# Causal masks on TensorE: eight 64 by 64 tiles per four banks in place of sixteen 32 by 32 tiles

## The chip, the cores and the metric

One core of a Trainium2 chip runs the whole program. The metric is the device time of one execution in microseconds. Three executions of the kernel before took 2279.23, 2272.83 and 2267.55 us; the median is 2272.83 us.

## What is computed

The input is x with 32 batches of 128 tokens by 512 values, and a context of the same shape. Per batch, four residual stages follow each other:

```python
x = x + wkv(w, u, layernorm(x), ctx)              # decayed running sums over the tokens
x = x + attention(layernorm(x))                   # 16 heads of 32, causal: s <= t only
x = x + mlstm(layernorm(x), ctx, ctx)             # 16 heads, causal matrix exp(log_D)
x = x + experts(layernorm(x))                     # top 8 of 32 experts
# attention: scores = where(causal, q k^T * scale, lowest); softmax over s
# mlstm:     log_D  = where(lower triangle, F_t - F_s + i_s, -inf)
```

The two `where` lines are what the change is about. A large negative number is put in PSUM at every place outside the triangle, and the scores are then added onto it.

## The kernel before, in words

**Two phases.** The first (about the first 1130 us) is a software pipeline over the batches: in step j, batch j is in stage 0, batch j-1 in stage 1, and so on up to stage 5. Steps 0 to 5 and 32 to 36 are written out, and steps 6 to 31 (26 of them) are one loop. The second phase runs the experts and has no masks.

**Order by hand.** The instructions of each engine within a step stand in an order fixed by hand (`step` of each engine), and the engines meet through semaphores. Every engine works strictly down its own list.

**Masks.** `masks(bank, mask)` (L1188 to L1194) fills four PSUM banks of 128 partitions by 512 values with the causal mask. It multiplies pieces of the identity with pieces of a mask table (bfloat16). Each matmul streams 512 columns: 128 columns of the table, repeated for four heads. A matmul that reads SBUF partitions of row group i and writes PSUM partitions of column group q uses only the corner (i, q) of the TensorE array. Before, there are four row groups and four column groups of 32, so the sixteen matmuls of one call use sixteen different corners. Bank r of column group q takes row group (q + r) mod 4, and the tables are turned by as much.

**Its three callers in a step**, in PE's order:
1. `scores` (L1247, stage 1): masks in banks 0 to 3, then 16 products of q and k (L1251). PE waits for `head_norm_ready` ahead of it (L1415, L1416). DVE's `row_max` (L1696) waits for its end, and PE goes on to `gates` (L1258) and `centre` (L1264).
2. `scores_turned` (L1279, stage 1): masks in banks 0 to 3, then L1283. `minus_max` (L1290), `v` (L1296 to L1298), `y_turn`, `row_sums` (L1306) and `weighted_v` (L1314) come after it on PE. ACT's four exponentials wait for `minus_max`.
3. `log_d` (L1317, stage 2): masks in banks 4 to 7, then four products (L1321). PE waits ahead of it for ACT's `lt_part`, for POOL's `spread_sums` (L618) and for ACT's `log_row_sums` (L1484, L1485). ACT's `exp_log_d3` (L939) waits for its end at L1129 (L1130 takes the semaphore down). `qk` (L1329) is PE's last work of the step.

**After that**, in the next step, PE waits for `exp_log_d3` (L1341, L1342), then does `z_turn` (L1164), `project` (L1201 to L1204) and the rest. POOL issues eight indirect DMAs (`store_pair`, L557) per step from step 5 on; the last three follow `spread_sums` directly.

Of the kernel before, what the change touches and what calls it, by code (L numbers as in the profile page):

```python
# [21 lines left out]
def build(nc, x, ctx_in, small, eye, fixed, fixed_half, gate_rows, Wa, Wp, ln_scale, gate_w, w_gate, w_up, w_down, out,  # L22
          NB=None, NE=None):
    B, T, D = x.shape
# [25 lines left out]
    with ExitStack() as whole:  # L50
# [6 lines left out]
        ps = whole.enter_context(nc.psum_tensor("ps", [P, 8, 512], F32))  # L57
# [29 lines left out]
        with ExitStack() as ctx:  # L87
# [21 lines left out]
            identb, ustrict = half_t[:, 0:P], half_t[:, P:2 * P]  # L109
# [1046 lines left out]
            def _(pe):  # L1156
# [29 lines left out]
                                  start=True, stop=True)  # L1186

                def masks(bank, mask):  # L1188
                    for q_ in range(4):
                        for r in range(4):  # L1190
                            i = slice(32 * ((q_ + r) % 4), 32 * ((q_ + r) % 4) + 32)
                            pe.matmul(ps[32 * q_:32 * q_ + 32, bank + r, :], identb[i, i],
                                      mask[i, r, :].unsqueeze(1).to_broadcast([32, 4, T]),
                                      start=True, stop=False, skip_group_check=True)  # L1194

                def z_turn():
# [50 lines left out]
                def scores():  # L1247
                    masks(S_BANK, mask_ts)
                    for c in range(4):
                        for r in range(4):  # L1250
                            m = pe.matmul(ps[:, S_BANK + r, c * T:(c + 1) * T], qs[32 * r:32 * r + 32, c, :],  # L1251
                                          ks[32 * r:32 * r + 32, c, :], start=False, stop=True, skip_group_check=True)
                    return m
# [25 lines left out]
                def scores_turned():  # L1279
                    masks(S_BANK, mask_st)  # L1280
                    for c in range(4):
                        for r in range(4):
                            m = pe.matmul(ps[:, S_BANK + r, c * T:(c + 1) * T], ks[32 * r:32 * r + 32, c, :],  # L1283
                                          qs[32 * r:32 * r + 32, c, :], start=False, stop=False, skip_group_check=True)
                    return m
# [32 lines left out]
                def log_d():  # L1318
                    masks(LD_BANK, mask_st)
                    for r in range(4):  # L1320
                        m = pe.matmul(ps[:, LD_BANK + r, :], Lt[32 * r:32 * r + 32, :],  # L1321
                                      Rt[32 * r:32 * r + 32, :, :].rearrange("p c t -> p (c t)"),
                                      start=False, stop=True, skip_group_check=True)
                    return m
# [1294 lines left out]
def fixed_tables(np, bi, bf):  # L2619
    h, dh = bi.shape[0], 32  # L2620
    rows = np.arange(P)
    q, n = rows // 32, rows % 32
    cols = np.arange(P)
    pick = np.zeros((P, 4, P), np.float32)
    gsel = np.zeros((P, 2, P), np.float32)
    cmat = np.zeros((P, P), np.float32)
    bmat = np.zeros((P, 4, dh + 1), np.float32)
    side = np.zeros((P, 9), np.float32)
    for p in range(P):
        if n[p] < 4:  # L2630
            pick[p, n[p], :] = 1.0
        for r in range(4):
            for j in range(8):
                for m in range(2):
                    if n[p] == h * m + r + 4 * (j % 4):
                        gsel[p, m, 32 * r + j] = 1.0
        cmat[p, 32 * q[p]:32 * q[p] + dh - 1] = -1.0 / dh
        if n[p] < dh - 1:
            cmat[p, p] = 1.0 - 1.0 / dh
            bmat[p, q[p], n[p]] = 1.0  # L2640
            bmat[p, q[p], dh - 1] = -1.0
        else:
            bmat[p, q[p], dh] = 1.0
        if n[p] < 4:
            side[p, 0], side[p, 3] = 1.0, 1.0
        elif n[p] < 8:
            side[p, 1], side[p, 2] = 1.0, -1.0
        if n[p] < 8:
            side[p, 5 + n[p] % 4] = 1.0
    side[0:h, 4:5] = bi.reshape(h, 1)  # L2650
    side[h:2 * h, 4:5] = bf.reshape(h, 1)
    table = np.concatenate([pick.reshape(P, 4 * P), gsel.reshape(P, 2 * P), cmat, bmat.reshape(P, 4 * (dh + 1)), side], axis=1)
    one, low = 0x3F80, 0xF14A
    half = np.zeros((P, 10, P), np.uint16)
    half[rows, 0, rows] = one
    half[:, 1, :][cols[None, :] > rows[:, None]] = one
    for i in range(4):
        for r in range(4):
            for p in range(32):
                t = 32 * ((i - r) % 4) + p  # L2660
                half[32 * i + p, 2 + r, :][cols > t] = low
                half[32 * i + p, 6 + r, :][cols < t] = low
    return table, half.reshape(P, 10 * P)


# [34 lines left out]
```

How the kernel before makes its waits and increments, by code:

```python
            def scale_rows(eng, k, part, step):  # L433
                part_of = [[wdst[:, (part + j) // 2, ((part + j) % 2 * 2 + n) * P:((part + j) % 2 * 2 + n + 1) * P]
                            .rearrange("p (h d) -> p h d", h=H) for n in range(2)] for j in range(2)]
                for j in range(2):
                    eng.tensor_tensor(scaled_heads(k, j)[:, :, 0:DS], main_columns(k, j), scale(j, 0, DS), ALU.mult)
                    eng.tensor_tensor(part_of[j][0], low_columns(k, 1 - j), scale(j, 1, R), ALU.mult)
                    a = eng.tensor_tensor(part_of[j][1], low_columns(k, j), scale(j, 2, R), ALU.mult)
                a.then_inc(step, 1)
                eng.wait_ge(step, 1)
                eng.sem_inc(step, -1)
                for j in range(2):
                    a = eng.tensor_tensor(scaled_heads(k, j)[:, :, DS:DH], part_of[j][0], part_of[j][1], ALU.add)
                return a
# [23 lines left out]
                def load_x(i):  # L470
                    sp.wait_ge(first_residual_ready_for_sp, 1)
                    sp.sem_inc(first_residual_ready_for_sp, -1)
                    sp.dma_start(xt[:, :], x[bass.ds(i, 1)].rearrange("a p d -> p (a d)")).then_inc(x_loaded, 16)
# [1 line left out]
                def load_ctx(i):  # L475
                    sp.wait_ge(ctx_turn_ps, 1)
                    sp.sem_inc(ctx_turn_ps, -1)
                    sp.dma_start(ct[:, :], ctx_in[bass.ds(i, 1)].rearrange("a p d -> p (a d)")).then_inc(ctx_loaded, 16)
```

## Time and profile before

| what | value |
|---|---|
| median of three executions | 2272.83 us |
| the profiled execution | 2280.1 us |
| its span, first to last instruction | 2278.3 us |
| PE busy | 2008.4 us (88%) |
| DVE, ACT, POOL busy | 1581.6, 1203.3, 1534.6 us |
| mean granted TensorE clock | 0.964 |

The profiled execution is 7.3 us above the median of the three; 1.8 us of it lie outside the span. A line of the trace names the engine, the line of the kernel, the operation and the tiles. A number in square brackets behind it is the time the engine sat idle just before, with what ended it: `PEq L1416` is PE's own instruction queue, which was waiting at line 1416. The granted clock is 1.00 at 2.4 GHz and 0.50 at 1.2 GHz.

### The profile page before, as it was taken

What the parts mean: (1) busy time and instruction counts of PE and PEld (TensorE: products, weight loads), DVE (VectorE), ACT (ScalarE), POOL (GpSimd) and SP (SyncE); (2) the same over time, 40 slices, a digit from 0 to 9 for tenths busy, and PEclk for the clock granted to TensorE, in tenths of its full rate; (3) what the DMA queues carried; (4) which work ended last, traced back from release to release, by engine and by line L of the source; (5) the groups of instructions that cost most, each with busy time, mean ns of one, the idle gap of its engine ahead of it and who ended that gap; (6) DMA issues with size and microseconds to landing.
All of it is one profiled execution on the core that took longest, in us unless ns stands there. A gap on an engine that the chain in (4) does not pass through costs nothing. (4 is left out here: it accounts for less than half of the span.)

```text
span 2278.3 us, 66587 instructions
## 1 busy us (share of the span) xinstructions
PE 2008.4 (88%) x22279; PEld 1459.6 (64%) x22280; DVE 1581.6 (69%) x3262; ACT 1203.3 (53%) x3018; POOL 1534.6 (67%) x1622
## 2 busy tenths in 40 slices
PE   2899999999899899998748999999999999999986
PEld 2676666666666666666426776676776777767664
DVE  6688877877777777876445775777666667666663
ACT  3576556566656655665424554555454445554542
POOL 4247766766766776776667777777776777776764
PEclk9999999999999999999869999999999999999998
DMA  3111001001101000001028787777887878786874
GB/s 118 44 39 39 28 28 37 28 28 37 30 25 37 31 29 33 33 28 40 20 59 175 165 183 157 166 166 155 177 170 165 165 166 179 166 169 134 180 143 79
DMA packets 136030, 219.47 MB, mean 96 GB/s; under 512 B 28032, under 2 KB 61184, under 8 KB 135936
## 3 DMA queue, kind: packets, MB, share of 16 engines
q0 software_dynamic: 73472, 139.82, 32.0%
q1 hardware_dynamic: 57856, 70.17, 9.8%
q10 hardware_dynamic: 4608, 8.39, 1.0%
q8 instruction: 39, 0.64, 0.1%
q14 instruction: 55, 0.45, 0.1%
HBM read 133.07 MB, written 96.73 MB: 101 GB/s over the span
## 5 line engine op out<-in xcount | busy, mean ns | idle before, releaser
L2268 POOL DMA_INDIRECT out_dram<-y,m_add x300 | 498.4, 1661 | 218.1 <-POOLq L2276 156.4
L2418 PE MATMUL ps<-xh,wh 128*128 128x256 f16 (+1 forms) x1752 | 381.4, 267 | 6.4 <-PEq L2430 4.7
L2419 PE MATMUL ps<-xh,wl 128*128 128x256 f16 (+1 forms) x1752 | 381.4, 267 | 1.6 <-issue 1.6
L557 POOL DMA_INDIRECT slot_scratch<-pair,slots x248 | 295.0, 1190 | 79.2 <-issue 55.8
L2260 POOL DMA_INDIRECT xg<-z_scratch,slot_t x260 | 264.5, 1017 | 84.6 <-issue 75.6
L2499 ACT ACTIVATE y<-ps,wts_now 128x512 f32<-128x512 f32 x294 | 185.5, 682 | 148.0 <-ACTq L2498 123.5
L2423 PE MATMUL ps<-xl,wh 128*128 128x256 f16 (+1 forms) x1752 | 229.0, 267 | 2.5 <-PEq L2434 2.0
L2573 DVE SCALAR_TENSOR_TENSOR hx<-ps,s 64x256 f16<-64x256 f32 x146 | 62.2, 426 | 235.4 <-issue 131.1
L2418 PEld LDWEIGHTS ps<-xh,wh 128*128 128x128 f16 x1752 | 171.8, 98 | 52.8 <-issue 24.3
L2515 ACT ACTIVATE xh<-ps 128x512 f16<-128x512 f32 x146 | 87.2, 597 | 217.6 <-ACTq L2514 184.8
L2419 PEld LDWEIGHTS ps<-xh,wl 128*128 128x128 f16 x1752 | 171.8, 98 | 29.4 <-issue 0.8
L2423 PEld LDWEIGHTS ps<-xl,wh 128*128 128x128 f16 x1752 | 164.4, 98 | 24.4 <-issue 6.5
L2380 PE MATMUL ps<-ident,xg 128*128 128x128 f32 x1040 | 136.5, 275 | 31.0 <-DMA xg<-z_scratch,slot_t 27.3
L2398 PE MATMUL ps<-dh,hx 128*128 128x512 f16 x294 | 112.4, 382 | 41.5 <-PEq L2395 37.5
L2380 PEld LDWEIGHTS ps<-ident,xg 128*128 128x128 f32 x1040 | 116.9, 141 | 35.6 <-DMA xg<-z_scratch,slot_t 28.4
L2582 DVE CAST xh<-ps 128x512 f16<-128x512 f32 x146 | 100.0, 685 | 31.8 <-DVEq L2581 24.8
L2574 DVE SCALAR_TENSOR_TENSOR h<-ps,s 64x256 f32<-64x256 f32 (+1 forms) x292 | 121.5, 416 | 0.0
L2406 PE MATMUL ps<-dh,hh 128*128 128x512 f16 x294 | 113.7, 387 | 7.8 <-PEq L2403 3.4
L2590 DVE TENSOR_TENSOR xl<-ps,xh 128x512 f16<-128x512 f32 x146 | 100.9, 691 | 21.5
L2522 ACT ACTIVATE s<-ps 64x256 f32<-64x256 f32 x146 | 55.1, 378 | 113.0 <-ACTq L2521 102.0
L2407 PE MATMUL ps<-dl,hh 128*128 128x512 f16 x294 | 113.8, 387 | 0.0
L2401 PE MATMUL ps<-dl,hx 128*128 128x512 f16 x294 | 112.6, 383 | 0.0
(342 smaller groups left out, 5165.3 us busy)
## 6 DMA issues: line engine op xcount, KB each, us to landing
wst<-in_L_ffn_w_gate_dram SPq DMA_DIRECT2D x32, 384.0 KB
wst<-in_L_ffn_w_up_dram SPq DMA_DIRECT2D x32, 384.0 KB
xt<-in_x_dram SPq DMA_DIRECT2D x32, 256.0 KB
ct<-in_ctx_dram SPq DMA_DIRECT2D x32, 256.0 KB, 2.6
out_dram<-x SPq DMA_DIRECT2D x32, 256.0 KB
z_scratch<-zn ACTq DMA_DIRECT2D x32, 256.0 KB, 2.0
wdst<-in_L_ffn_w_down_dram SPq DMA_DIRECT2D x32, 256.0 KB
out_dram<-y,m_add POOLq DMA_INDIRECT x300
```

What stands on the lines that cost most here:

```text
L557: pool.indirect_dma_start(out=slot_d[:, :], out_offset=bass.IndirectOffsetOnAxis(ap=slots[:, k:k + 1], axis=0), in_=pair[:, k, :], in_offs ...
L2260: pool.indirect_dma_start(out=xg[b][:, h, :], out_offset=None, in_=z_d[:, :], in_offset=bass.IndirectOffsetOnAxis(ap=rows(h), axis=0)).the ...
L2268: pool.indirect_dma_start(out=acc_d[:, :], out_offset=bass.IndirectOffsetOnAxis(ap=m_add[:, k, h:h + 1], axis=0), in_=y[:, k, h, :], in_of ...
L2380: m = pe.transpose(ps[:, bank, c0:c0 + P], xg[b][:, h, k * P:(k + 1) * P], ident[:, :])
L2401: pe.matmul(o, hx2[:, t], dl[:, j, 1, :], start=False, stop=False)
L2406: pe.matmul(o, hh1[:, t], dh[:, j, 0, :], start=False, stop=False)
L2407: pe.matmul(o, hh1[:, t], dl[:, j, 0, :], start=False, stop=False)
L2418: pe.matmul(ps[:, dst, 0:cols], wh[:, j, k, c0:c0 + P], xh[:, k, 0:cols], start=(k == 0), stop=False)
L2419: pe.matmul(ps[:, dst, 0:cols], wl[:, j, k, c0:c0 + P], xh[:, k, 0:cols], start=False, stop=False)
L2423: m = pe.matmul(ps[:, dst, 0:cols], wh[:, j, k, c0:c0 + P], xl[:, k, 0:cols], start=False, stop=(k == KC - 1))
L2499: act.activation(y[:, k, h, :], ps[:, 5 + h, :], ACT.Copy, scale=wts_now[:, h:h + 1])\
L2574: dve.scalar_tensor_tensor(full, up, 1.0 / WSC, s, ALU.mult, ALU.mult).then_inc(dve_step, 1)
```

## The change

The loops run over two row groups and two column groups of 64 in place of four and four of 32. One call still fills four whole banks, with eight matmuls, each with 512 columns. The mask tables, built on the host, are turned to match; their size stays as it was. Nothing else differs.

```diff
                 def masks(bank, mask):
-                    for q_ in range(4):
+                    for q_ in range(2):
                         for r in range(4):
-                            i = slice(32 * ((q_ + r) % 4), 32 * ((q_ + r) % 4) + 32)
-                            pe.matmul(ps[32 * q_:32 * q_ + 32, bank + r, :], identb[i, i],
-                                      mask[i, r, :].unsqueeze(1).to_broadcast([32, 4, T]),
+                            i = slice(64 * ((q_ + r) % 2), 64 * ((q_ + r) % 2) + 64)
+                            pe.matmul(ps[64 * q_:64 * q_ + 64, bank + r, :], identb[i, i],
+                                      mask[i, r, :].unsqueeze(1).to_broadcast([64, 4, T]),
                                       start=True, stop=False, skip_group_check=True)
...
-    for i in range(4):
+    for i in range(2):
         for r in range(4):
-            for p in range(32):
-                t = 32 * ((i - r) % 4) + p
-                half[32 * i + p, 2 + r, :][cols > t] = low
-                half[32 * i + p, 6 + r, :][cols < t] = low
+            for p in range(64):
+                t = 64 * ((i - r) % 2) + p
+                half[64 * i + p, 2 + r, :][cols > t] = low
+                half[64 * i + p, 6 + r, :][cols < t] = low
```

## Rows read from the trace of the kernel before

**Rows 1.** The page, first part: busy time of each engine.

```profile
PE 2008.4 (88%) x22279; PEld 1459.6 (64%) x22280; DVE 1581.6 (69%) x3262; ACT 1203.3 (53%) x3018; POOL 1534.6 (67%) x1622
```

**Rows 2.** Windows: stretch, length, busy (count) by engine, PE clock, DMA share, GB/s.

```profile
240.00:1080.00 840.00, 764.47 (x11161) 543.69 (x11145) 639.99 (x1342) 500.11 (x1287) 578.53 (x795) 0.95 0.10 32
...
624.55:627.95 3.40, 3.40 (x11) 1.17 (x10) 2.92 (x7) 3.02 (x10) 1.13 (x3) 0.50 0.20 77
523.75:527.10 3.35, 3.35 (x19) 1.89 (x20) 3.00 (x7) 3.23 (x12) 1.22 (x2) 1.00 0.21 79
220.90:224.00 3.10, 3.10 (x19) 1.61 (x17) 3.10 (x8) 2.98 (x10) 0.96 (x3) 1.00 0.22 85
```

**Rows 3.** One line's instructions: row_max (L1696) in the loop of 26 steps.

```profile
L1696 DVE TENSOR_REDUCE nm<-ps x26: 2290/2292/2294, 204.2 to 1048.2; 128x16 f32<-128x2048 f32 x26
```

**Rows 4.** Timeline of DVE, row_max of six steps: start, length, idle before.

```profile
204.16 2.29 DVE L1696 TENSOR_REDUCE nm<-ps 128x16 f32<-128x2048 f32 x1 [1.04 <-DVEq L2024]
236.50 2.29 DVE L1696 TENSOR_REDUCE nm<-ps 128x16 f32<-128x2048 f32 x1 [1.03 <-DVEq L2024]
...
508.12 2.29 DVE L1696 TENSOR_REDUCE nm<-ps 128x16 f32<-128x2048 f32 x1 [1.04 <-DVEq L2024]
539.76 2.29 DVE L1696 TENSOR_REDUCE nm<-ps 128x16 f32<-128x2048 f32 x1 [1.05 <-DVEq L2024]
573.69 2.29 DVE L1696 TENSOR_REDUCE nm<-ps 128x16 f32<-128x2048 f32 x1 [1.04 <-DVEq L2024]
607.72 2.29 DVE L1696 TENSOR_REDUCE nm<-ps 128x16 f32<-128x2048 f32 x1 [1.05 <-DVEq L2024]
```

**Rows 5.** Timeline of PE in one step of the loop.

```profile
605.88 0.44 PE L1192 MATMUL ps<-half_t 32*32 32x512 bf16 x16 [0.76 <-PEq L1416]
606.25 1.17 PE L1251 MATMUL ps<-ks,qs 32*128 32x128 f32 x32
...
610.93 0.43 PE L1192 MATMUL ps<-half_t 32*32 32x512 bf16 x16
611.30 1.17 PE L1283 MATMUL ps<-qs,ks 32*128 32x128 f32 x32
...
613.39 0.38 PE L1296 MATMUL ps<-wvh,xnh 128*128 128x512 f16 x1
613.61 0.38 PE L1297 MATMUL ps<-wvl,xnh 128*128 128x512 f16 x1
...
618.92 0.44 PE L1192 MATMUL ps<-half_t 32*32 32x512 bf16 x16 [0.35 <-PEq L1485]
619.29 1.14 PE L1321 MATMUL ps<-Rt,Lt 32*128 32x512 f32 x8
620.50 1.59 PE L1329 MATMUL ps<-qT,kT 32*128 32x128 f32 x26
...
624.05 0.63 PE L1164 MATMUL ps<-ident,zn 128*128 128x128 f32 x4 [0.62 <-PEq L1342]
```

**Rows 6.** Timeline of ACT and POOL in the same step.

```profile
623.16 0.60 ACT L939 ACTIVATE dm<-ps 128x512 f32<-128x512 f32 x1 [2.09 <-ACTq L1130]
...
617.58 1.04 POOL L618 TENSOR_TENSOR Rt<-nx,fixed_t 128x512 f32<-128x512 f32 x1
...
620.16 0.96 POOL L557 DMA_INDIRECT slot_scratch<-pair,slots  x1 [0.30 <-issue]
621.43 0.96 POOL L557 DMA_INDIRECT slot_scratch<-pair,slots  x1 [0.30 <-issue]
```

**Rows 7.** Timeline of PE: start of qk and of z_turn in two other steps.

```profile
216.94 0.94 PE L1329 MATMUL ps<-qT,kT 32*128 32x128 f32 x21
...
220.52 0.63 PE L1164 MATMUL ps<-ident,zn 128*128 128x128 f32 x4 [0.52 <-PEq L1342]
...
520.91 1.57 PE L1329 MATMUL ps<-qT,kT 32*128 32x128 f32 x28
...
523.75 0.63 PE L1164 MATMUL ps<-ident,zn 128*128 128x128 f32 x4 [0.52 <-PEq L1342]
```

## The prediction, made before the changed kernel ran

> **What bounds the kernel now.** I read the page first: PE is busy 88% of the span [rows 1]. Masks are laid only in the first phase, so I cut out its loop of 26 steps. PE is busy 764 of 840 us there, and the granted clock averages 0.95, not 1.00 [rows 2]. The reader is to see two things: PE has little idle time to give, and its clock is not always full. Next come the step lengths, from one `row_max` to the next. 26 of them start between 204.2 and 1048.2 us [rows 3], so 25 intervals average 33.76 us. They are of three kinds [rows 4]: 34.03 us (573.69 to 607.72), 31.64 us (508.12 to 539.76) and 32.34 us (204.16 to 236.50). In the first kind the clock is 0.50 for 3.4 us at the start of `project`; in the other two it is 1.00 at that place [rows 2]. Going through the loop step by step I find two intervals of the short kind and one of the middle kind; from the mean of 33.76 the other 22 then average 34.0. With the last step that makes 23 low stretches, which agrees with the mean clock: 0.95 over 840 us, rounded, stands for 22 to 27 stretches of 3.4 us at 0.50 [rows 2].
>
> What sets the end of a step I take from the timelines [rows 5, 6]. PE waits 0.76 us before `scores`, 0.35 before `log_d` and 0.62 before `z_turn`. The striking one is ACT: the four products of `log_d` are streaming from 619.29, and `qk` follows at 620.50, yet ACT waits for the end of `log_d` until 623.16, after 2.09 us idle. POOL's last two indirect DMAs run from 620.16 to 622.39 in that time. Whatever holds the release back, it comes some 2 us after the arithmetic, and the next step (`z_turn` at 624.05) hangs on it.
>
> **The price of one call.** Sixteen matmuls start almost together: one lasts about 0.38 us and the group 0.44, so the last starts 0.06 after the first. The next group starts 0.37 after the first start, in all three calls [rows 5]. That is one round of 512 columns (0.215 us between 512-column matmuls, 613.39 to 613.61) plus about 0.1 us of changing over. In the changed code the corners of the array come in this order, as (row group, column group): (0,0) (1,0) (0,0) (1,0) (1,1) (0,1) (1,1) (0,1). If starts keep program order, the third has to wait for the first; the fifth and sixth go with the third and fourth; the seventh waits for the fifth. That makes three rounds in place of one: two more at 0.215, less 0.05 since fewer starts follow each other in the last round. I take +0.38 us per call. The bounds: one round, if nothing conflicts, -0.03; two rounds +0.17; all eight in a row +1.45 (seven more times 0.215, less 0.05).
>
> A rule that bears on this: the Trainium skill, "TensorEngine Tiling (Array Packing)", Tiling Modes, gives the array four independent tiles at 64 by 64. Eight matmuls would then be two rounds, +0.17 us per call. The Trainium skill, "TensorE: Matmul & The Clock Gate", Part 3, says that matmuls start in program order; by that it is three. The trace agrees with the latter only so far as no matmul in it starts ahead of an earlier one; no row has a call in which a corner is used twice.
>
> **Where the calls stand.** *First call (`scores`).* PE starts it when a wait ends, and DVE waits 1.05 us for its end [rows 4]. `gates` and everything DVE, ACT and POOL do for the gates come after it, down to POOL's `spread_sums` at 617.58 and the indirect DMAs behind it [rows 6]. So +0.38 passes to the whole step. The least is 0 (if `head_norm` came earlier, which nothing gives), the most 0.38.
>
> *Second call (`scores_turned`).* PE has no idle time around it, so `minus_max`, `v`, the exponentials, `row_sums` and with them ACT's logarithm, for which PE waits before `log_d`, are 0.38 later. *Third call (`log_d`).* Another 0.38. Both together put the products of `log_d` from 619.29 to 620.05 (counted without the first call), and their end to about 621.2. That is still ahead of 623.16, when ACT went on [rows 6]. `qk` moves from 620.50 to about 621.25; at its pace without gaps (L1251, 1.17 us for the same work) it would end at 622.4. The cover is the late release, nearly 2 us of it. POOL's DMAs do not wait for these two calls. I take 0 for both; if the cover is gone, 0.76 per step. Below nothing is open too: in the step at 508.12 `z_turn` came 2.84 us after `qk` started, against 3.55 in the common step [rows 5, 7], so a release 0.7 us earlier occurs.
>
> *Count.* 26 steps of the loop times 0.38 is 9.9 us. Outside it there are 96 - 78 = 18 calls. In steps 1 to 4 no indirect DMA runs, so nothing hides the 11 calls there. Of the 7 others I count 5 (the first of step 5, three of step 32, one of step 33). 16 times 0.38 is 6.1. Sum +16.0 us. The host's tables have the same size and cost nothing; 24 fewer matmuls per step shorten only PE's queue.
>
> **The clock.** A low stretch costs 34.0 - 32.34 = 1.65 us. Before it, PE is sparse: `qk` starts at 620.50, runs with gaps, and `z_turn` starts at 624.05. The second and third call push the dense work 0.75 us into that hole. The distance from `qk` to `z_turn` becomes about 2.8 us, as in the step at 508.12 that kept its clock (2.84). Against that, the step at 204.16 kept its clock with 3.58 [rows 7]. So the hole alone does not decide, and its place in time counts too. None of the 23 stretches or all of them may go: 0 to -38 us. I take 8, since neither end has more than a row or two for it: -13.2 us.
>
> **Sum.** +16.0 - 13.2 = +2.8 us, on 2280.1 us for the profiled execution. That one stands 7.3 us above the median; on 2272.83 it makes 2275.6 us.
>
> **Rivals.**
> - *Forecast, mixed clock.* Between 2 and 14 stretches go: +12.7 to -7.1, or 2266 to 2286 us. Chance 0.34.
> - *Slower: the clock falls as often as now.* Place: the hole before `z_turn`. Price: the full +16.0, 2288.8 us; and, if the cover of the second and third call is gone in the loop, 52 times 0.38 more (+19.8), 2308.6 us. It decides when fewer than 3 stretches go, or when 0.3 us of the two later calls passes to each step. For it: the hole begins later but ends at the same semaphore, and steps 0.38 us longer may fall on low stretches just as often. Against it: denser PE work where the clock is decided. Chance 0.34.
> - *Faster: the clock holds.* All 23 go: 16.0 - 38.0 = -22 us, 2250.9. If the release also comes 0.7 us earlier in each step, because `log_d` ends at a better moment between POOL's DMAs, 2232.7. For it: the 2.84 us above, in a step of 31.64. Against it: two short steps in 25 are little. Chance 0.22.
> - *The change does not do what it says.* With two rounds, each passing call costs 0.17: 42 calls, +7.1 us; with 8 stretches gone, -6.1, or 2266.7 us. Chance 0.08. All eight in a row: 42 times 1.45, +61 us, 2334 us. For it speaks no row, since matmuls in different corners overlap now. Chance 0.02.
>
> **How the numbers follow.** A measurement of this kernel can tell about 0.5%, 11.4 us, from no change. Faster takes the third case and a part of the two rounds (0.25); the same, the forecast and the rest (0.39); slower, the second and the last (0.36). For 8 in 10 I leave out all eight in a row, the earliest release in every step, and the full loss of cover: 2248 to 2304 us. The likeliest case's own range is 2266 to 2286. The predicted time is 2276 us.
>
> **What would show it.** Eight L1192 matmuls of 64 by 64 per call in starts of 2, 4 and 2, about 0.215 apart, and the next group 0.75 after the first start (0.54 for two rounds). `qk` 0.7 to 0.8 us later against `row_max`, with ACT's wait at L1130 shorter by about as much and its end unmoved. Steps with a full clock of 32.7 us, with a low one 34.4. The number of stretches at 0.50 in the loop, 23 now, decides the sign: 15 is the forecast, 20 or more is slower, under 10 faster. The forecast is wrong in its mechanism if `qk` ends later against `spread_sums` by more than 0.3 us and `z_turn` with it, or if the calls keep to 0.4 us.

## The result, and the profile after

The changed kernel takes 2217.36 us, the median of four executions (2215.52 to 2220.25); the kernel before took 2276.03 us on the same chip (four executions, 2267.55 to 2282.05). The ratio is 0.9746, with a 95% interval of 0.9722 to 0.9771: 59 us faster, outside the range of the prediction on its fast side. The profiled execution took 2215.52 us, its span 2213.6 us, with a mean granted clock of 0.983.

The first part of the page after, against [rows 1]:

```profile
PE 1966.0 (89%) x21511; PEld 1438.6 (65%) x21512; DVE 1581.0 (71%) x3262; ACT 1206.7 (55%) x3018; POOL 1534.8 (69%) x1622
```

768 matmuls are gone (96 calls, eight fewer in each), and PE is busy 42 us less. DVE, ACT and POOL do what they did. Two windows of the loop, against [rows 2] (the second lies at the start of `project`, where the common step had its clock at 0.50):

```profile
240.00:1080.00 840.00, 766.23 (x11037) 551.93 (x11035) 666.74 (x1427) 526.86 (x1348) 614.70 (x857) 0.99 0.11 34
313.00:316.40 3.40, 3.38 (x18) 1.83 (x19) 2.28 (x5) 2.83 (x11) 1.44 (x3) 1.00 0.08 30
```

Of the 23 low stretches of the loop one is left. DVE, ACT and POOL do 4 to 6% more in the same 840 us: the steps are shorter. DVE's timeline, `row_max` of two steps, against [rows 4]:

```profile
298.17 2.29 DVE L1696 TENSOR_REDUCE nm<-ps 128x16 f32<-128x2048 f32 x1 [1.08 <-DVEq L2024]
329.25 2.29 DVE L1696 TENSOR_REDUCE nm<-ps 128x16 f32<-128x2048 f32 x1 [1.08 <-DVEq L2024]
```

31.08 us, where the common step had 34.03. From the first `row_max` of the loop to the one after the loop it was 878.4 us (204.2 to 1082.6) and is 817.1 us (205.0 to 1022.1). These 61.3 us are nearly all of the 64.6 between the two profiled executions. PE's timeline of that step, against [rows 5]:

```profile
301.36 0.63 PE L1192 MATMUL ps<-half_t 64*64 64x512 bf16 x8
301.92 1.17 PE L1283 MATMUL ps<-qs,ks 32*128 32x128 f32 x32
...
309.33 0.63 PE L1192 MATMUL ps<-half_t 64*64 64x512 bf16 x8 [0.34 <-PEq L1485]
309.90 1.14 PE L1321 MATMUL ps<-Rt,Lt 32*128 32x512 f32 x8
310.91 1.59 PE L1329 MATMUL ps<-qT,kT 32*128 32x128 f32 x32
313.02 0.79 PE L1164 MATMUL ps<-ident,zn 128*128 128x128 f32 x4 [0.52 <-PEq L1342]
```

Two things are to be seen. A call hands over after 0.56 us, not 0.37: the price is +0.19 us. And `qk` is no longer strung out: it takes 1.59 us where it took up to 3, and `z_turn` starts 2.11 us after it, not 3.55. ACT's and POOL's timelines of the same step, against [rows 6]:

```profile
312.13 0.60 ACT L939 ACTIVATE dm<-ps 128x512 f32<-128x512 f32 x1 [0.65 <-ACTq L1130]
```

```profile
308.00 1.04 POOL L618 TENSOR_TENSOR Rt<-nx,fixed_t 128x512 f32<-128x512 f32 x1
309.19 1.08 POOL L557 DMA_INDIRECT slot_scratch<-pair,slots  x1 [0.16 <-issue]
310.58 0.96 POOL L557 DMA_INDIRECT slot_scratch<-pair,slots  x1 [0.30 <-issue]
```

ACT now goes on 4.13 us after `spread_sums` began; before it was 5.58 us (623.16 less 617.58). In both kernels three indirect DMAs follow `spread_sums`; the view above shows the first two, [rows 6] the last two. Measured from the end of `log_d`'s last product (the profile models the ends of matmuls), the release comes 0.95 us late (median of 26 steps) where it came 2.60 us late. ACT's waits at L1130 in the loop, first of the kernel before, then after (total us, times, longest):

```profile
ACT dm L939 <- ACTq L1130: 52.7, 26, 2.1
```

```profile
ACT dm L939 <- ACTq L1130: 20.3, 25, 2.0
```

So the late release, which the prediction used as cover, is what shrank.

### The profile page after: what moved, and what is told of

Read it like the earlier page. It is cut to its first block and busy times, and to the rows that moved or that the text cites. A ratio compares the mean times of both kernels' runs of the same rounds, so it can differ in the third digit from the quotient of the medians.

```text
span 2213.6 us, 65051 instructions
## 1 busy us (share of the span) xinstructions
PE 1966.0 (89%) x21511; PEld 1438.6 (65%) x21512; DVE 1581.0 (71%) x3262; ACT 1206.7 (55%) x3018; POOL 1534.8 (69%) x1622
```

## Experiments

The runs were made in five series, each with the kernel before beside it: 1 (e1, e3, e4, e7), 2 (e2, e5, e6, e8), 3 (c1 and the runs with f), 4 (with g), 5 (with h). The series fell on two conditions of the machine, and this matters for all that follows. In series 1 and 3 the kernel before took 2283.6 and 2281.6 us, as in the first measurement. In series 2, 4 and 5 it took 2130.6, 2130.1 and 2129.2 us. The first are called **slow-release** series, the others **prompt-release** series, after what their traces show. "Lag" is the time from the end of `log_d`'s last product to its semaphore; "qk" is the time from its first start to its last end; both are medians of the 26 loop steps. Low stretches are counted in the loop. Most expectations were written for a kernel before of 2280 us, and some name a kind of chip; chip 0 gave both series 3 (slow-release) and series 4 (prompt-release), so the number of the chip does not decide the condition. Where a run fell in a prompt-release series, what they say of releases and low stretches had no object, and only the price of the masks and of moved work could be read.

| run | ratio to before (95%) | step | lag | qk | low |
|---|---|---|---|---|---|
| *slow-release:* before, profiled | | 33.98 | 2.60 | 2.95 | 23 |
| changed, profiled | 0.9746 (0.9722 to 0.9771) | 31.08 | 0.95 | 1.56 | 1 |
| e1_split16 | 1.0001 (0.9970 to 1.0032) | 33.82 | 2.50 | 3.12 | 16 |
| e3_third64 | 0.9757 (0.9710 to 0.9803) | 31.17 | 1.01 | 1.62 | 1 |
| e4_moved | 0.9821 (0.9772 to 0.9869) | 31.65 | 0.04 | 1.17 | 1 |
| e7_shift | 1.0025 (1.0001 to 1.0050) | 34.06 | 2.39 | 3.04 | 20 |
| c1_changed | 0.9801 (0.9761 to 0.9841) | 31.64 | 1.73 | 2.32 | 0 |
| f5_firsttwo64 | 1.0069 (1.0032 to 1.0105) | 34.06 | 2.71 | 3.13 | 25 |
| f8_split16b | 1.0039 (0.9998 to 1.0080) | 34.07 | 2.48 | 3.12 | 18 |
| f2_whole4 | 0.9908 (0.9879 to 0.9936) | 32.33 | see there | 1.07 | 0 |
| *prompt-release:* g0_changed | 1.0011 (0.9997 to 1.0024) | 29.79 | 0.04 | 1.17 | 0 |
| e5_firsttwo64 | 1.0015 (1.0002 to 1.0028) | 29.72 | 0.04 | 1.17 | 0 |
| e8_split16b | 1.0017 (1.0003 to 1.0031) | 29.69 | 0.04 | 1.17 | 0 |
| e2_whole4 | 1.0143 (1.0120 to 1.0166) | 30.41 | 0.04 | 1.07 | 0 |
| g1_changed_moved | 1.0194 (1.0163 to 1.0225) | 31.27 | 0.04 | 1.17 | 0 |

### Is it the tiles or the number of matmuls?

The 64 by 64 tiles stay, but each matmul is cut into two of 256 columns, so that a call has sixteen again. In e1 both halves carry the start flag, and its masks do not stay whole under the scores. In e8 and f8 (one edit, two series; the diff) only the first half carries it, and the masks stay whole.

```diff
-                            pe.matmul(ps[64 * q_:64 * q_ + 64, bank + r, :], identb[i, i],
-                                      mask[i, r, :].unsqueeze(1).to_broadcast([64, 4, T]),
-                                      start=True, stop=False, skip_group_check=True)
+                            for h_ in range(2):
+                                pe.matmul(ps[64 * q_:64 * q_ + 64, bank + r, 256 * h_:256 * h_ + 256], identb[i, i],
+                                          mask[i, r, :].unsqueeze(1).to_broadcast([64, 2, T]),
+                                          start=(h_ == 0), stop=False, skip_group_check=True)
```

> The changed kernel with each 64 by 64 mask matmul cut in two of 256 columns: sixteen matmuls per call again, the same tiles and the same columns in all. Theory A (the number of TensorE instructions ahead of qk is what counts: qk and the release of log_d are held up by a supply or completion path that falls behind while POOL issues its indirect DMAs): the gaps in qk come back, qk takes 2.4 to 2.9 us from its first start to its last end instead of about 1.5, the release of log_d lags its arithmetic by over 2 us in most steps, loop steps are above 33 us and the kernel is within 0.7% of the kernel before. Theory B (tile shape and array work count: larger tiles keep the clock and shorten what follows): steps stay at 31.0 to 31.2 us and the kernel at 2215 to 2222 us.

> As e1_split16, but only the first of the two halves of a bank carries the start flag, so that the masks stay whole. Theory A: as there, the lag of the release about 2.5 us and qk about 3.1 us in most steps, 2265 to 2285 us. If the time of e1_split16 came from its second start flags and not from the count, this one is as fast as the changed kernel, 2215 to 2225 us.

> The kernel of e8_split16b again (64 by 64 tiles, each matmul cut in two of 256 columns, sixteen per call). On a chip of the first kind, theory A: lag about 2.5 us, qk about 3.1 us, within 0.7% of the kernel before; theory B: as fast as the changed kernel. On a chip of the second kind: 1.000 to 1.003.

PE's timeline of a step of e1, then DVE's `row_max` of two pairs of steps:

```profile
313.80 0.66 PE L1193 MATMUL ps<-half_t 64*64 64x256 bf16 x16 [0.27 <-PEq L1483]
314.38 1.14 PE L1322 MATMUL ps<-Rt,Lt 32*128 32x512 f32 x8
315.38 0.90 PE L1330 MATMUL ps<-qT,kT 32*128 32x128 f32 x18
316.48 0.47 PE L1330 MATMUL ps<-qT,kT 32*128 32x128 f32 x2 [0.20 <-issue]
317.20 0.51 PE L1330 MATMUL ps<-qT,kT 32*128 32x128 f32 x5 [0.26 <-issue]
317.96 0.52 PE L1330 MATMUL ps<-qT,kT 32*128 32x128 f32 x7 [0.25 <-issue]
```

```profile
237.84 2.29 DVE L1697 TENSOR_REDUCE nm<-ps 128x16 f32<-128x2048 f32 x1 [1.10 <-DVEq L2025]
270.25 2.29 DVE L1697 TENSOR_REDUCE nm<-ps 128x16 f32<-128x2048 f32 x1 [1.10 <-DVEq L2025]
...
469.36 2.29 DVE L1697 TENSOR_REDUCE nm<-ps 128x16 f32<-128x2048 f32 x1 [1.12 <-DVEq L2025]
503.43 2.29 DVE L1697 TENSOR_REDUCE nm<-ps 128x16 f32<-128x2048 f32 x1 [1.14 <-DVEq L2025]
```

The call takes 0.58 us, practically as in the changed kernel, on the same corners and with the same columns, and still the whole gain is gone, in e1 and in f8. Tiles and array time are not the cause; the number of matmuls (each with its weight load) is. The rows also show a second sign of it: `qk` runs 18 products without a gap and then comes in driblets, with idle time that no wait explains ("issue"). Counted from the first mask on, PE got 16 + 8 + 18 = 42 matmuls without a gap. In the changed kernel `qk` comes to its first such gap (over 0.18 us from one start to the next) after 26 to 31 products in most steps of the two slow-release traces, in the step shown after 29, which is 8 + 8 + 29 = 45; the idle time behind it is short, so the view shows all 32 as one group of 1.59 us. The eight matmuls saved are eight to thirteen products more before PE is held up.

The `row_max` rows part the two costs. 32.41 us is a step of e1 with the late release and the clock at 1.00; 34.07 is one with the late release and a low stretch. So a low stretch costs 1.66 us, and a lag of 2.5 us in place of the changed kernel's 0.95 costs 32.41 - 31.08 = 1.33 us. The rest of the lag costs nothing here: four steps of e1 that have no late release at `log_d` at all take 31.13 to 31.23 us, no less than the 31.08.

### Which of the three calls?

Tables of both shapes are kept, so that one call can change without the others. The diff is e3's (its other calls keep sixteen tiles). e3 has 64 by 64 in `log_d` alone; e5 and f5 have it in `scores` and `scores_turned` alone.

```diff
                 def log_d():
-                    masks(LD_BANK, mask_st)
+                    masks(LD_BANK, mask_st64)
```

> Only the third call (log_d) uses eight 64 by 64 tiles; scores and scores_turned keep sixteen of 32 by 32. Theory A with a short memory (only the instructions just ahead of qk count): nearly all of the gain stays, and the two other calls are 0.2 us cheaper each, so steps of 30.7 to 31.0 us and a kernel of 2205 to 2222 us. Theory A with a long memory, or a gain that comes from the first two calls: steps over 32 us and a kernel above 2240 us. Theory B predicts something between, about a third of the gain, near 2255 us.

> The converse of e3_third64: scores and scores_turned use eight 64 by 64 tiles, log_d keeps sixteen of 32 by 32. Theory A with a short memory: no gain at log_d, lag about 2.6 us and qk about 2.9 us, two calls 0.19 us dearer each, 2270 to 2295 us. If fewer instructions 5 to 13 us ahead of log_d help as well: lag under 1.5 us and below 2240 us.

> The kernel of e5_firsttwo64 again (log_d keeps sixteen tiles of 32 by 32, the two other calls have eight of 64 by 64). On a chip of the first kind, theory A with a short memory: lag about 2.6 us, qk about 2.9 us, within 1% of the kernel before. If the two earlier calls help too: lag under 1.5 us and 2240 us or less. On a chip of the second kind: as before, 1.000 to 1.003.

PE's and ACT's timelines, of e3 first:

```profile
306.59 0.63 PE L1195 MATMUL ps<-half_t 64*64 64x512 bf16 x8 [0.35 <-PEq L1495]
307.15 1.14 PE L1331 MATMUL ps<-Rt,Lt 32*128 32x512 f32 x8
308.16 1.53 PE L1339 MATMUL ps<-qT,kT 32*128 32x128 f32 x32
...
309.41 0.60 ACT L941 ACTIVATE dm<-ps 128x512 f32<-128x512 f32 x1 [0.69 <-ACTq L1132]
```

and of f5:

```profile
555.26 0.44 PE L1202 MATMUL ps<-half_t 32*32 32x512 bf16 x16 [0.28 <-PEq L1492]
555.62 1.14 PE L1331 MATMUL ps<-Rt,Lt 32*128 32x512 f32 x8
556.83 0.90 PE L1339 MATMUL ps<-qT,kT 32*128 32x128 f32 x18
557.96 0.40 PE L1339 MATMUL ps<-qT,kT 32*128 32x128 f32 x3 [0.23 <-issue]
...
559.58 0.60 ACT L941 ACTIVATE dm<-ps 128x512 f32<-128x512 f32 x1 [2.19 <-ACTq L1132]
```

The split is clean: the third call alone brings all of it (0.9757), the first two alone bring nothing and cost 0.7%. It is not fewer matmuls anywhere in the step, it is fewer of them between PE's wait at L1485 and `qk`. In f5 nearly every step is low (25), and ACT waits as long as before.

### Is it only that `log_d` sits elsewhere in time?

A single dense filler ahead of the masks moves `log_d` and leaves the rest of the kernel before as it was.

```diff
                 def log_d():
+                    keep_busy(LD_BANK, 1)
                     masks(LD_BANK, mask_st)
```

> The kernel before with one more matmul of 128 by 128 and 512 columns in front of the masks of log_d, so that its products start 0.2 to 0.35 us later, as they do in the changed kernel, with one instruction more instead of eight fewer. Theory C (only the moment at which log_d ends against POOL's DMAs counts): the release comes early and the gain of the change shows, below 2235 us. Theory A: nothing gained, 2265 to 2290 us, since there are no fewer instructions. Theory B: a small gain at most, from the busier array ahead of the low clock.

`log_d` starts 0.3 us later (11.87 against 11.58 us after `row_max`), and nothing is gained: lag 2.39, 20 low stretches, 1.0025. A shift as such does not free the release.

### What does POOL have to do with it?

In e4 the kernel before issues its last three indirect DMAs of a step in the next one, after `hold_ctx`, away from `log_d` and `qk`.

```diff
                     if on(1):
                         hold_ctx().then_inc(hold_ctx_ready, 1)
+                    if on(6):
+                        store_pair(4)
+                        store_pair(5)
+                        store_pair(6)
...
-                    if on(5):
-                        store_pair(4)
-                        store_pair(5)
-                        store_pair(6)
```

> The kernel before, with 32 by 32 tiles, but POOL's last three indirect DMAs of a step are issued in the next step, after hold_ctx, so none runs beside log_d and qk. If they are what holds up the release (in every theory where POOL's DMAs are a partner): log_d's release lags its arithmetic by under 0.1 us, qk has no gaps and ends about 1.3 us after its first start, the clock stays at 1.00 before project, and steps are 30 to 31.5 us: 2190 to 2225 us. If the hold-up is TensorE's own (the instruction supply alone): gaps and release stay as before, steps 33 to 34 us, 2265 to 2285 us.

PE's timeline of a step, with ACT's first exponential and POOL's first moved DMA:

```profile
280.89 0.44 PE L1196 MATMUL ps<-half_t 32*32 32x512 bf16 x16 [0.35 <-PEq L1489]
281.26 1.14 PE L1325 MATMUL ps<-Rt,Lt 32*128 32x512 f32 x8
282.41 1.17 PE L1333 MATMUL ps<-qT,kT 32*128 32x128 f32 x32
...
282.88 0.58 ACT L943 ACTIVATE dm<-ps 128x512 f32<-128x512 f32 x1
...
283.75 0.63 PE L1168 MATMUL ps<-ident,zn 128*128 128x128 f32 x4 [0.17 <-PEq L1346]
...
285.57 1.08 POOL L557 DMA_INDIRECT slot_scratch<-pair,slots  x1 [0.16 <-issue]
```

With sixteen 32 by 32 tiles, the lag is gone (ACT does not wait), `qk` runs through in 1.17 us, and 22 of 23 low stretches are gone; the one that is left lies elsewhere, 10 us after the start of `qk` in the last step. The late release needs POOL's indirect DMAs beside it, and it moves with them: in e4 the semaphore of `head_sums` (L1217), which runs beside the moved DMAs, comes 1.40 us late (median, in all 26 steps), where no trace without the move has it late. e4 is still slower than the changed kernel: its step is 31.65 us. Two reasons are open beside each other, these new late releases, and the three DMAs standing in the way of other work; the second must be worth something, since g1 (below) pays 1.5 us per step for the same move where nothing is released late.

The same count over the other semaphores of PE shows that `log_d` is not the only place. `gates` (L1258) is released 1.13 us late before and 0.96 us late in the changed kernel, and the step's first `head_product` (L1179) 1.24 and 1.23 us late (medians, in at least 25 of 26 steps each). In no prompt-release trace is one of them 0.1 us late. ACT waits for `gates`; its lines, first before, then the changed kernel, then the changed kernel in a prompt-release series (g0):

```profile
609.21 0.37 ACT L878 ACTIVATE gates_part<-ps,fixed_t 128x128 f32<-128x128 f32 x1 [2.81 <-ACTq L1060]
```

```profile
299.64 0.37 ACT L878 ACTIVATE gates_part<-ps,fixed_t 128x128 f32<-128x128 f32 x1 [2.83 <-ACTq L1060]
```

```profile
298.27 0.37 ACT L878 ACTIVATE gates_part<-ps,fixed_t 128x128 f32<-128x128 f32 x1 [1.90 <-ACTq L1060]
```

That is 1.49, 1.47 and 0.55 us after the start of `row_max` of the step. So the change shortens one of three late releases and leaves the other two nearly as they are.

### Four whole matmuls, the other loop order

e2 and f2 lay the masks by four matmuls of 128 by 128 per call; e6 is the changed kernel with the loops over `r` and `q_` swapped, so that a corner comes a second time only after all four have been used.

```diff
+                    for r in range(4):
+                        pe.matmul(ps[:, bank + r, :], identb[:, :], mask[:, r, :].unsqueeze(1).to_broadcast([P, 4, T]),
+                                  start=True, stop=False, skip_group_check=True)
```

> Four matmuls of 128 by 128 per call, no tiling, unturned tables: four rounds of 512 columns, 0.43 us more per call than the changed kernel, and four instructions fewer. Theory A with the saving already had: the lag is at or under 0.95 us and qk at 1.2 to 1.6 us; the first call passes its 0.43 us on, the others pass some of it, steps 31.3 to 32.0 us, 2222 to 2250 us. If the count still saves at the rate of the change (16 fewer instructions gave 2.7 us): 2190 to 2215 us.

> The kernel of e2_whole4 again (four matmuls of 128 by 128 per call). On a chip of the first kind: against the changed kernel four instructions fewer per call and 0.43 us more of array time; lag at or under 0.95 us, steps 31.3 to 32.0 us, 2222 to 2250 us. On a chip of the second kind: 1.012 to 1.017.

> The changed kernel with the loops over bank and column group swapped, so that the first four matmuls use four different corners of the array and the last four use them again. If starts keep program order and a corner must be free, this order needs two rounds where the changed kernel's needs three: its products start 0.2 us sooner after the masks. If both orders take two rounds: 0.56 us from first start to the next group in both, and 2215 to 2225 us.

PE's timeline of a step of f2, and DVE's division by the row sums:

```profile
221.15 1.02 PE L1190 MATMUL ps<-half_t 128*128 128x512 bf16 x4
222.11 1.14 PE L1318 MATMUL ps<-Rt,Lt 32*128 32x512 f32 x8
...
223.71 0.69 DVE L1756 TENSOR_TENSOR oT<-ps,rinv 128x512 f32<-128x512 f32 x1 [1.95 <-DVEq L2108]
...
224.66 1.17 PE L1326 MATMUL ps<-qT,kT 32*128 32x128 f32 x32 [1.42 <-ACTq L1126]
```

A call now takes 0.96 us, 0.40 more than eight matmuls, and in prompt-release conditions that alone is 1.0143. In slow-release conditions it still beats the kernel before (0.9908), with no low stretch, but not the changed one. This step shows a turn that the lag at `log_d` doesn't: the late release is now that of `weighted_v`, whose end is at 221.02; its semaphore comes 2.45 us later, and DVE waits for it until 223.71 (this is so in 8 of the 26 steps). So what is held up is not tied to `log_d`, but to whatever PE finishes in that time. In e6 the next group starts 0.556 us after the first (0.563 in the changed kernel) and its one execution took 2131.78 us, where before took 2130.58: the order does not matter.

### The change repeated, and versions of it

> The changed kernel itself, beside the kernel before on one chip. On the chip of the first series the kernel before took 2283.6 us and its kin showed the late release (lag 2.5 us); on that of the second series it took 2130.6 us and no kernel there had a late release. If this chip is of the first kind (the kernel before near 2280): ratio 0.970 to 0.979, lag near 0.95 us, steps of 31.1 us. If it is of the second kind (near 2130): the change has nothing to remove, its 0.19 us in the first call remains, so 1.000 to 1.004.

> The changed kernel, as the control of this series. On a chip of the first kind (the kernel before near 2280 us): 0.972 to 0.984, lag of the release 0.9 to 1.8 us, no stretch of low clock in most of the loop. On one of the second kind (2130): 1.000 to 1.004.

c1 and g0 are the changed kernel. c1, in slow-release conditions, gives 0.9801: the gain is there again, though the lag is 1.73 us in most steps and not 0.95. g0, in prompt-release conditions, gives 1.0011 (0.9997 to 1.0024): no difference. Its step, by the timelines of PE and ACT:

```profile
308.29 0.63 PE L1192 MATMUL ps<-half_t 64*64 64x512 bf16 x8
308.85 1.14 PE L1321 MATMUL ps<-Rt,Lt 32*128 32x512 f32 x8
309.94 1.17 PE L1329 MATMUL ps<-qT,kT 32*128 32x128 f32 x32
...
310.41 0.58 ACT L939 ACTIVATE dm<-ps 128x512 f32<-128x512 f32 x1
...
311.28 0.63 PE L1164 MATMUL ps<-ident,zn 128*128 128x128 f32 x4 [0.17 <-PEq L1342]
```

There is no late release to shorten, although POOL's DMAs stand beside `log_d` as before (their starts are at 308.15, 309.53 and 310.79). What is left of the change is the price of the masks, 2 us or so in 2130.

g1 is the changed kernel with e4's edit, g2 and h2 move only the last of the three DMAs, and g3 and h3 put eight matmuls of 32 columns ahead of `log_d`'s masks, to ask whether the count alone decides.

```diff
                 def log_d():
+                    for _ in range(8):
+                        pe.matmul(ps[:, LD_BANK, 0:32], identb[:, :], mask_ts[:, 0, 0:32], start=True, stop=True)
                     masks(LD_BANK, mask_st)
```

> The changed kernel with POOL's last three indirect DMAs moved into the next step as in e4_moved. If the lag that is left in the changed kernel has the same partner: lag under 0.1 us, qk 1.17 us; steps set by the other work. e4_moved had 31.65 us in steps without any lag, against 31.1 to 31.6 in the changed kernel, so the three DMAs cost something in their new place: 31.3 to 31.9 us, 2220 to 2245 us, not a gain over the changed kernel. If the instruction count is all and the DMAs only a marker: lag stays at 0.9 or more.

> The changed kernel with only the last of the three indirect DMAs moved. The release in the changed kernel comes during or just after the third. Without it there: lag 0.0 to 1.0 us, qk under 1.6 us in all steps; one DMA in the new place costs a third of what three do. Steps 30.7 to 31.2 us, 2200 to 2222 us, faster than the changed kernel; if the place of the DMA costs as much as it saves, 2215 to 2232 us.

> The kernel of g2_changed_moved1 again, for a chip of the first kind (the kernel before near 2280 us). There the changed kernel stood at 0.975 and 0.980. If the lag left in it comes from the last of the three DMAs: lag 0.0 to 1.0 us, below 0.972. If not: 0.972 to 0.985, lag 0.9 to 1.8 us. On a chip of the second kind: 0.998 to 1.002, as in g2.

> The changed kernel with eight tiny matmuls (32 columns, 128 by 128) in front of the masks of log_d: the instruction count ahead of qk is that of the kernel before, the array work hardly changes. Theory A: lag back at 2.3 to 2.7 us, qk about 3 us, low clock in over half of the steps, within 1% of the kernel before. If instead the number of matmuls that write the four banks, or the masks' own shape, counts: lag and time of the changed kernel plus at most 0.3 us per step.

> The kernel of g3_padded again, for a chip of the first kind. Theory A, the count as such: lag 2.3 to 2.7 us, qk about 3 us, 0.993 to 1.010. If the masks' own shape counts: lag and time of the changed kernel, 0.975 to 0.990. On a chip of the second kind: 1.001 to 1.004, as in g3.

All five fell in prompt-release conditions, where the question can't be asked. g1 took 1.0194 (1.0163 to 1.0225): the moved DMAs cost 1.5 us per step, with nothing to win. g2 and h2 were level with before (0.9998 and 1.0002), g3 and h3 0.2% above it (1.0022, 1.0010 to 1.0035; 1.0016, 1.0004 to 1.0027). Whether eight tiny matmuls bring the late release back, and whether g2 helps where it is late, stays open. No version was found that beats the changed kernel; e3 equals it within the interval.

## Why the prediction was wrong

**The step that failed** is the half sentence "24 fewer matmuls per step shorten only PE's queue", which put the count of matmuls at nothing without a reason. Eight of the 24, those ahead of `log_d`'s products, made all of the gain (e3, f5), and by their number, not their tiles or columns (e1, f8). The runs show for it 22 low stretches fewer (36.3 us) and steps that are 1.33 us shorter at the same clock. With it fell the use of the late release as fixed cover: "whatever holds the release back", the prediction took it to come when it came. It moves: the lag is 0.95 us for 2.60.

**Two rounds, not three.** The price of a call is +0.19 us, half of the +0.38 taken, and lies near the bound of two rounds (+0.17). In the trace the eight starts of a call lie at 0, 4, 14, 17, 215, 244, 254 and 257 ns; the third and fourth use a corner that the first and second still occupy, and are on record as started all the same. The total of 0.563 us is that of two rounds; "starts keep program order" gave the wrong number of rounds. By the four independent tiles of the Trainium skill, "TensorEngine Tiling (Array Packing)", Tiling Modes, it is two; the measured time agrees with that.

**Where the calls stand.** The delay of the first two calls arrives as forecast in kind: `minus_max` starts 4.74 us after `row_max`, 4.57 before. The whole price per step is small: 2 to 4 us of 2130 where nothing else differs (g0 +0.11%, e8 +0.17%), against 42 times 0.19 = 8.0 us by the prediction's own count with the right price. Less than half of it shows; which of the calls is covered was not parted.

**The clock.** The price of a low stretch was right: 1.65 us forecast, 1.66 in e1. The number that goes was not: 8 forecast, 22 measured. The rule that the prediction sought, and left at "the hole alone does not decide", is half of the answer. I divided the steps by the length of `qk` in the nine slow-release traces other than f2 (26 steps each):

```text
                         qk over 2.8 us   of them low   other steps   of them low
before                        24              23             2             0
changed                        1               1            25             0
e1_split16                    22              16             4             0
e3_third64                     1               1            25             0
e4_moved                       0               0            26             1
e7_shift                      24              20             2             0
c1_changed                     1               0            25             0
f5_firsttwo64                 25              25             1             0
f8_split16b                   24              18             2             0
sum                          122             104           112             1
```

A strung-out `qk`, with `z_turn` 3.4 us or more after its start, goes with a fall to 1.2 GHz in 104 steps of 122; a more compact one, with `z_turn` at 1.2 to 2.9 us, in 1 of 112. The hole does not force the fall, but without it there is hardly one. What parts the 18 steps that kept the clock from the 104 is open. Two short steps in 25 were read as too little; they were the two in which the release came earlier (lag 1.9 us).

**The sum by measured terms.** 22 low stretches less: 22 x 1.65 = -36.3 us. Release earlier: 19 steps of about 31.08 in place of 32.41, -25.3; five of 31.55, -4.3; against that the two steps of before that were already short, +1.6. The masks make a step with late release and full clock 32.41 where [rows 4] has 32.34: 24 x 0.07 = +1.7. The one long step of the loop, 35.21 for 35.05, +0.2; its last step, 33.62 for 34.42 less 1.65, +0.85. Together -61.6, measured -61.3. These terms are read from the steps that they are to explain, so the sum shows only that nothing large is missing.

**The rivals.** "The clock holds" had the direction and, with the release 0.7 us earlier, 2232.7 us. With its terms set right (price halved, +8.0; clock, -38.0; 1.33 us per step, -34.6) it comes to 2208.2 us, 9 below the measured 2217.36. Its reason, that `log_d` ends at a better moment between POOL's DMAs, is not supported: e7 moved the moment and gained nothing, f8 kept the moment of the changed kernel and lost everything. "Two rounds" had the price. The sign that would prove the forecast wrong, `qk` ending elsewhere against `spread_sums`, came on the side that the text didn't name, earlier: the end of `qk` lies 312.50 - 308.00 = 4.50 us behind the start of `spread_sums`; before it was 5.85 (620.50 [rows 5] and 2.93 us of `qk`, less 617.58 [rows 6]).

## What to carry to other kernels

Count the instructions of an engine behind a wait, not only their time, where its trace has idle time that ends at nothing ("issue") in the middle of a plain run of matmuls; there, half as many matmuls with more array time can win. A release that comes long after the arithmetic is an effect to be explained, not a cover to be spent: look for the steps in which it isn't late, and ask what they lack. And repeat a gain at another time: this one is 2.5% in one condition of the machine and nothing in the other, and one chip gave both.

## What the runs showed that was not expected

- **Two conditions, 7% apart.** The same kernel before took about 2280 us in three measurements and 2130 us in three others, with spreads of 0.5 to 1.2% in each. The runs traced in the second have no late release (lag 0.04 us), no broken `qk`, no low stretch in the loop; the kernel before itself was not traced there, but e5 is, whose `log_d` is the same. What sets the condition is open. It acts on more than the masks and the loop: between the changed kernel's two traces, after and g0, 41.6 us of the difference lie in the loop and 41.9 us behind it, where no masks are laid.
- **A DVE instruction three times as long is no sign of the condition.** L1704, the same 128 by 508 values, takes 2.1 us in nine of the ten slow-release traces and 0.68 us in nine of the ten prompt-release ones; f2 and e2 are the other way round. First DVE and POOL before, then DVE in g0:

```profile
610.96 2.10 DVE L1704 SCALAR_TENSOR_TENSOR cv<-cv,sp_ 128x508 f32<-128x508 f32 x1
611.22 1.29 POOL L600 TENSOR_TENSOR x<-x2k,hw 128x512 f32<-128x512 f32 x1
```

```profile
300.53 0.68 DVE L1704 SCALAR_TENSOR_TENSOR cv<-cv,sp_ 128x508 f32<-128x508 f32 x1
```

  In all twenty traces together it is long in each of the 251 steps in which POOL's L600 runs beside it, and short in each of the 389 others. In g0 POOL's L600 starts at 301.50, after L1704.
- **PE stops after a count.** Behind the wait ahead of `log_d`, PE runs 41 to 48 matmuls (masks, `log_d`'s products and `qk`) before its first such gap, in nearly all late-release steps (37 in the one long step of the loop), in before, the changed kernel, e1, e3, f5 and e7 alike, whether their masks are sixteen or eight, and then goes on in groups of two to seven. That POOL's indirect DMAs are needed for it is shown by e4. How the two are coupled, and whether it is the supply of PE's instructions or something else, is not shown; the run that would have asked whether the count alone decides, g3, never met the late release. That in f2 a semaphore comes 2.45 us late while PE goes on working speaks for more than a lack of instructions.
- **The lag takes few values.** Single steps of the same run have no lag at all, with `qk` at 1.17 us (one in the changed kernel, four in e1), or one of a few fixed values: 0.95 or 1.62 us in the changed kernel, 1.0 or 1.73 in c1.
